# Two-layer transformer block: the first feed-forward run batch by batch, with the second attention's norm, projections and row maxima placed beside it and beside the first batch's values

## The chip, the cores and the metric

The kernel is one program on 1 core of a Trainium2 chip. The metric is the device time of one execution in microseconds, as the median of several runs. The kernel before was timed in 3 runs. A profiled execution of it gives the rows shown below.

## What is computed

Two layers work on x, 2 batches of 512 tokens by 256 features. Each layer is `x += gate * attention(norm(x))` and then `x += gate * ffn(norm(x))`, where the gates and the scale and shift of each norm come from a small vector c per batch.

```python
# layer 0 attention: 16 heads of 16, causal window of 64 tokens
scores = where(band, q @ k.T / 4, -max);  out = softmax(scores) @ v;  out @ w_out.T
# layer 0 ffn: a shared expert and 16 routed experts (4 chosen of 2 groups)
y = sum_e combine[t, e] * (silu(x @ W1[e].T) * (x @ W3[e].T)) @ W2[e].T
# layer 1 attention: 16 query heads, ONE key head and ONE value head, causal over all 512 tokens
# layer 1 ffn: a shared expert of 1024 and 8 routed experts of 128 (2 chosen)
```

All products are float32 in quality: each operand is split into a high part (rounded) and a low part (the rest), and a product is three matmuls, hi*hi, lo*hi and hi*lo.

## The kernel before

Each engine has its program written out by hand; semaphores join them. The order of the work is the order of the code, and no scheduler changes it.

**Feed-forward.** The hidden units of a layer are cut into tiles of 128: 25 tiles in layer 0, 16 in layer 1. A tile's weights are one 128x768 block. SyncE (SP) loads it into one of two raw buffers (`load_ffn`, L348), ScalarE (ACT) writes the high part (`weights_high`, L1288), GpSimd (POOL) the low part (`weights_low`, L519), and the next load into that buffer waits for the low part (`split`). A unit u is one tile for one batch. TensorE does `up(u)`, 12 matmuls of 128x512 in two halves (6 for g, 6 for u, L553), and one unit later `down(u)`, 12 matmuls of 128x256 (L994). Between them stand: ACT silu of g (L1308); VectorE (DVE) times u, which it reads from PSUM (L1783, "gu"); DVE times the combine row (L1786, "hid", both inputs in SBUF); ACT high part (L1312, "high"); DVE low part (L1790, "low"). `down(u)` waits for "low". A tile serves batch 0 and then batch 1, so the weights of a layer are loaded and split once, every second unit. The first three tiles ("early") run while the norm of batch 1 is still under way.

**After the feed-forward of layer 0.** `causal_maxima` follows: the norm of layer 1, `project1` (q, k, v), then for 32 heads (16 per batch) `scores` on TensorE (L724 and mask products L729), three row maxima on DVE (L1572) and a masked copy of q on ACT (L1160). The maxima of a batch are transposed (`max_rows`, L747), split by ACT and DVE, and stored to DRAM (L304, `store_maxima`) as two more rows of q; SP then loads q rows pair by pair of heads into four slots (L372).

**Values.** `values_pass(1)` makes, for 16 pairs of heads in three thirds each (48 steps j), `keys_major(j)` (scores with the keys on the partitions, L846, with the maximum already subtracted by those two rows), exp on ACT (L1228), and for each group of four heads four value products (L877). DVE reads a group's result, divides and transposes (L1588 to L1605), POOL makes its low part (L496), and `project_out` (L892) multiplies by the output weights. In steps of it ACT makes the high parts of the first three tiles of layer 1's feed-forward, at j = 11, 17 and 25, and SP loads the next raw tiles after the q rows of heads u = 19 and u = 23 of the list of 32 (`load_attention`).

Batch 0 and batch 1 of the maxima stand before all values, so DRAM stores and loads of batch 0 lie beside the maxima of batch 1.

## Time and profile before

| what | us |
|---|---|
| median of 3 runs | 650.18 |
| lowest and highest run | 646.22, 654.21 |
| span of the profiled execution | 648.5 |
| TensorE busy in the span | 599.5 |
| VectorE busy | 379.0 |
| ScalarE busy | 302.4 |
| GpSimd busy | 118.5 |

The profiled execution has no time of its own beside its span: 648.5 us, 1.7 under the median of the runs. Busy TensorE is not TensorE at its peak, since the ends of matmuls are modelled. PEclk is the granted clock as a share of 2.4 GHz, so 0.50 is 1.2 GHz.

### The profile page before, as it was taken

The page shows a single profiled execution, that of the slowest core. Times are in us where ns is not written, and L with a number is a line of the kernel's source. Part 1 is how long each engine was busy: PE and PEld are TensorE (multiplying, and loading weights), DVE is VectorE, ACT ScalarE, POOL GpSimd, SP SyncE. Part 2 cuts the span into 40 slices and gives each one's busy share as a digit, 9 for nine tenths or more (in the row PEclk, how much of TensorE's full clock was granted, in tenths as well). Part 3 has the DMA queues.
Part 4 walks back from the last instruction along what each step waited for, and adds up shares of the span by engine and source line. Part 5 has one row for each costly group of instructions (what it writes and reads, how often), then busy time and mean ns, then how long its engine had stood idle before and what let it go on. Part 6 is the DMA issues. An engine that isn't in the chain of part 4 may idle for free.

```text
span 648.5 us, 10714 instructions
## 1 busy us (share of the span) xinstructions
PE 599.5 (92%) x3880; PEld 470.2 (73%) x3890; DVE 379.0 (58%) x757; ACT 302.4 (47%) x466; POOL 118.5 (18%) x90
## 2 busy tenths in 40 slices
PE   3899999898999999999999797889999999999995
PEld 3778645786888888888887565544446878888885
DVE  7567757753254544454457799795376543335556
ACT  3666775463233333333342583448855643333331
POOL 4500031223022222112230000001301231222220
PEclk9998999999699999999999899899999999999999
DMA  8454674000011111111100024402310000111101
GB/s 319 123 213 135 221 215 132 1 25 24 2 36 42 45 49 49 49 49 49 49 25 1 0 71 134 127 4 77 113 40 1 25 25 25 50 49 49 48 2 65
DMA packets 22195, 44.66 MB, mean 69 GB/s; under 512 B 3632, under 2 KB 7632, under 8 KB 22160
## 3 DMA queue, kind: packets, MB, share of 16 engines
q1 hardware_dynamic: 21840, 44.05, 21.5%
q8 instruction: 23, 0.38, 0.2%
q10 hardware_dynamic: 320, 0.13, 0.1%
q14 instruction: 12, 0.10, 0.0%
HBM read 33.16 MB, written 11.01 MB: 68 GB/s over the span
## 4 chain that ended last, share of the span: by engine, by line
PE 67%; DVE 19%; ACT 6%; issue 3%; DMA 3%; POOL 1%; SPq 1%; DVEq 0%; ACTq 0%
PE PS L553 32%; PE PS L994 15%; DVE nmx L1572 5%; PE PS L877 4%; DMA qk_slot<-rows_scr 2%; PE PS L846 2%; PE PS L825 2%; PE PS L830 2%; DVE stats L1470 1%; PE PS L724 1%; DVE x L1641 1%; DVE xn L1786 1%; PE PS L892 1%; PE PS L713 1%; PE PS L561 1%
## 5 line engine op out<-in xcount | busy, mean ns | idle before, releaser
L1312 ACT ACTIVATE qk_hi<-xn 128x512 fp32r<-128x512 f32 x82 | 51.7, 631 | 170.5 <-DVE xn L1786 140.8
L553 PE MATMUL PS<-h_hi,wqkv_hi 128*128 128x512 f32 x304 | 104.4, 401 | 2.6 <-DVE h_lo L1504 1.9
L553 PE MATMUL PS<-h_hi,wqkv_lo 128*128 128x512 f32 x272 | 92.3, 395 | 1.8 <-DVE xn L1696 1.8
L1783 DVE TENSOR_TENSOR prs<-prs,PS 128x512 f32<-128x512 f32 x60 | 41.2, 687 | 88.7 <-PE PS L553 77.7
L519 POOL TENSOR_TENSOR wqkv_hi<-fw_raw,wqkv_hi 128x768 fp32r<-128x768 f32 x18 | 33.1, 1841 | 254.3 <-ACT wqkv_hi L1288 254.3
L1790 DVE TENSOR_TENSOR qk_lo<-xn,qk_hi 128x512 fp32r<-128x512 f32 x70 | 48.4, 692 | 49.1 <-ACT qk_hi L1312 49.1
L1308 ACT ACTIVATE prs<-PS 128x512 f32<-128x512 f32 x82 | 48.5, 592 | 47.3 <-PE PS L553 47.3
L553 PEld LDWEIGHTS PS<-h_hi,wqkv_hi 128*128 128x128 f32 x304 | 58.1, 191 | 15.3 <-DVE h_lo L1504 2.7
L553 PE MATMUL PS<-h_lo,wqkv_hi 128*128 128x512 f32 x160 | 63.6, 397 | 0.0
L553 PEld LDWEIGHTS PS<-h_hi,wqkv_lo 128*128 128x128 f32 x272 | 51.1, 188 | 13.3 <-DVE xn L1696 2.7
L1572 DVE TENSOR_REDUCE nmx<-PS 128x512 f32 (+4 forms) x96 | 54.2, 635 | 4.6 <-PE PS L729 4.5
L994 PE MATMUL PS<-wqkv_hi,qk_hi 128*128 128x256 f32 x280 | 52.1, 285 | 0.9 <-POOL qk_lo L525 0.7
L519 POOL TENSOR_TENSOR wqkv_lo<-fw_raw,wqkv_lo 128x768 fp32r<-128x768 f32 x16 | 29.5, 1846 | 122.4 <-ACT wqkv_lo L1288 122.4
L553 PE MATMUL PS<-h_lo,wqkv_lo 128*128 128x512 f32 x128 | 50.3, 393 | 0.0
L994 PEld LDWEIGHTS PS<-wqkv_hi,qk_hi 128*128 128x128 f32 x280 | 45.0, 188 | 5.0 <-POOL qk_lo L525 1.6
L994 PE MATMUL PS<-wqkv_lo,qk_hi 128*128 128x256 f32 x256 | 47.3, 283 | 0.7 <-DVE qk_lo L1790 0.7
L1786 DVE TENSOR_TENSOR xn<-prs,V 128x512 f32<-128x512 f32 x60 | 44.7, 745 | 2.1
L994 PEld LDWEIGHTS PS<-wqkv_lo,qk_hi 128*128 128x128 f32 x256 | 41.0, 188 | 4.0 <-DVE qk_lo L1790 1.5
L994 PE MATMUL PS<-wqkv_hi,qk_lo 128*128 128x256 f32 x140 | 39.5, 282 | 0.0
L1566 DVE TENSOR_REDUCE nmx<-PS 128x384 f32 (+1 forms) x64 | 31.1, 548 | 13.0 <-PE PS L713 12.9
L994 PE MATMUL PS<-wqkv_lo,qk_lo 128*128 128x256 f32 x128 | 36.0, 281 | 0.0
L1160 ACT ACTIVATE q_masked<-qk_hi,headmask 128x512 fp32r<-128x512 f32 (+1 forms) x48 | 32.3, 715 | 5.5 <-PE PS L729 3.5
(259 smaller groups left out, 1203.2 us busy)
## 6 DMA issues: line engine op xcount, KB each, us to landing
fw_raw<-in_ffn SPq DMA_DIRECT2D x41, 384.0 KB, 3.1
qk_slot<-rows_scr SPq DMA_DIRECT2D x32, 200.0 KB
rows_scr<-qk_hi SPq DMA_DIRECT2D x16, 256.0 KB
qk_slot<-q_scr SPq DMA_DIRECT2D x32, 100.0 KB
rows_scr<-qk_lo SPq DMA_DIRECT2D x8, 256.0 KB
wmod<-in_wmod SPq DMA_DIRECT2D x1, 1536.0 KB, 13.4
x<-in_x SPq DMA_DIRECT2D x2, 512.0 KB, 4.1
wmod<-in_wmod SPq DMA_DIRECT2D x1, 1024.0 KB, 9.6
```

The source lines that it names most:

```text
L519: nc.gpsimd.tensor_tensor(w[1], fw[s][:, :], w[0].bitcast(F32), ALU.subtract)\
L553: ins = nc.tensor.matmul(dst, left(a, c), right(b, c), start=n == 0, stop=n == total - 1)
L877: ins = nc.tensor.matmul(PS[s * VW:s * VW + rows, O_BANK[l][g % 2], kb * P:kb * P + n], v, probs[l][slot][:, col:col + n], start=kb == 0, ...
L994: ins = nc.tensor.matmul(PS[:, 2 * b + t // 2, (t % 2) * D:(t % 2 + 1) * D], hidR[u % 2 if isinstance(u, int) else b][a][:, t * P:(t + 1) ...
L1160: nc.scalar.activation(qm[s][:, :], rows[:, bass.ds(head // 2, 1), :].rearrange("p m t -> p (m t)").bitcast(F32), ACT.Copy, scale=headmask ...
L1308: nc.scalar.activation(gact[b], PS[:, 4, :], ACT.Silu).then_inc(f["silu"], 1)
L1312: nc.scalar.activation(hidR[b][0], hid[b], ACT.Copy).then_inc(f["hi"], 1)
L1566: nc.vector.tensor_reduce(nmx[:, bass.ds(NT * u + 2 * i, 2)], PS[:, 2 * h + i, 0:2 * KEYS0].rearrange("p (t k) -> p t k", k=KEYS0), X, ALU ...
L1572: nc.vector.tensor_reduce(nmx[:, bass.ds(NT * u + qt, k)], PS[:, 3 * h + bank, 0:k * w].rearrange("p (t k) -> p t k", k=w), X, ALU.max, ne ...
L1783: tt(hid[buf] if half is None else gu[buf], gact[buf], PS[:, 5, :], ALU.mult).then_inc(f["gu"], 1)
L1786: tt(hid[buf], gu[buf], cB[b][half], ALU.mult).then_inc(f["hid"], 1)
L1790: tt(hidR[buf][1], hid[buf], hidR[buf][0].bitcast(F32), ALU.subtract).then_inc(f["lo"], 1)
```

## The change

**Layer 0's feed-forward runs batch by batch.** Units 0 to 27 are the early ones and batch 0; units 28 to 49 (`TURN` = 28) are batch 1. Every unit from 6 on has another tile, so tiles 3 to 24 are loaded and split twice: 47 loads for 25. Four pairs of buffers hold split weights (`fw0R`). On ACT the high part of a tile now stands between silu and "high" of every unit.

**Batch 0 of layer 1 stands beside batch 1's units.** The gates of layer 1 come after unit 9; half outputs and the norm of batch 0 in units 28 to 33; its projections in units 33 to 35; two heads of scores and maxima in each of units 37 to 44 (`FIRST_HEADS` = 37), all in one set of three PSUM banks (0, 1, 6); `max_rows` in unit 45.

**Batch 0's values come directly after.** Beside them stand batch 1's norm transposes (j = 8), projections (j = 12, 14, 15, 16) and heads 0 to 5 of its maxima (j = 18 to 23). Heads 6 to 15 follow alone, in two sets of banks; then `max_rows`, `project_out` of batch 0, and only then batch 1's values (j = 24 to 47), which need batch 1's maxima to have gone through DRAM. `keys_major` has two pairs of PSUM banks in turn where it had three. The first three tiles of layer 1's feed-forward are now split at j = 29, 35 and 41; SP still loads raw tiles behind heads u = 19 and u = 23. All filler matmuls of this part are gone, and the loops of layer 0's feed-forward are written out.

```diff
+MAX1_BANK = [7, 5]
+SCORE1 = [[(0, 1, 6)], [(2, 3, 7), (0, 1, 4)]]
+PAIR_BANK = [0, 4]
+ALONE = 6
...
-TAIL = [3, 2]
+TAIL = 2
 EARLY = 3
 EU = 2 * EARLY
+LAST0 = 2 * TILES[0]
+TURN = EU + TILES[0] - EARLY
+FIRST_HEADS = TURN + 9
...
+        fwX = [prxR[:, a, 0:TW] for a in range(2)]
+        fw0R = [fwR[0], fwR[1], fwX, fwE[1]]
...
+        def weights(l, i):
+            if l == 0:
+                return fw0R[i % 4]
+            return fwE[i % 2] if isinstance(i, int) and (2 <= i < 4 or i > TILES[1] - TAIL) else fwR[i % 2]
...
+        def tile0(j):
+            return j if j < TILES[0] else j - TILES[0] + EARLY
+        def heads_of(u):
+            i = 2 * (u - FIRST_HEADS)
+            return (i, i + 1) if 0 <= i < H else (None, None)
+        def scored1(b, i, piece):
+            sets = SCORE1[b]
+            if b and i >= ALONE:
+                return sets[i % 2][piece]
+            return sets[0][piece]
...
+            load_attention(0, 2 * SLOTS, UNITS)
+            load_ffn_rest(0)
+            rows_at = FIRST_HEADS + 4
+            load_ffn_again(TILES[0], rows_at)
+            store_rows1(0)
+            load_ffn_again(rows_at, rows_at + 1)
+            load_keys1(0)
+            load_ffn_again(rows_at + 1, LAST0 - EARLY)
+            store_maxima(sp, 1, 0)
+            load_attention(1, 0, H)
+            store_rows1(1)
+            load_keys1(1)
+            sp.wait_ge(ff[0]["split"], LAST0 - EARLY)
             for s in range(2):
                 load_ffn(1, 0, s, s)
-            store_maxima(sp, 1, 0)
-            sp.wait_ge(at[0]["st"], UNITS)
-            load_attention(1)
...
+            def attention1():
+                for c in range(CHUNKS):
+                    if c == 2:
+                        weights_low(1, 0, 0)
+                        weights_low(1, 1, 1)
+                    elif c == 3:
+                        weights_low(1, 2, 0)
+                    out_low(1, c)
...
+            for j in range(EARLY + 1, LAST0 - EARLY):
+                weights_low(0, j, j % 2)
+            attention1()
...
-                if u >= THIRDS:
-                    pe.wait_ge(a["p"], u - THIRDS + 1)
+                if u >= 2:
+                    pe.wait_ge(a["p"], u - 1)
+                if u == 0:
+                    pe.wait_ge(k1_loaded, 16 * 4)
+                    pe.wait_ge(a["mxd"], 3 * H)
+                elif u == 1:
+                    pe.wait_ge(ff[0]["silu"], LAST0)
+                    pe.wait_ge(ff[0]["gu"], LAST0 - EU)
+                elif u == THIRDS * PAIRS // 2:
+                    pe.wait_ge(k1_loaded, 16 * 4 * B)
+                    pe.wait_ge(a["mxd"], 3 * UNITS)
...
+            def beside_first_values(j):
+                if j == 8:
+                    norm_transposes(2, (1,))
+                elif j in (12, 14, 15, 16):
+                    project1(1, {12: 2, 14: 0, 15: 1, 16: 3}[j])
+                elif j in (18, 19, 20, 21, 22, 23):
+                    if j == 18:
+                        pe.wait_ge(qhi, 4 * B + 6)
+                        pe.wait_ge(v1_taken, 2)
+                    scores1(1, j - 18)
+            def beside_last_values(j):
+                if j == 37:
+                    norm_transposes(3, (0,))
+            def values_pass1(b, beside):
+                first = b * THIRDS * PAIRS // 2
+                for j in range(first + 2 * (1 - b), first + 6):
+                    keys_major(1, j)
+                for g in range(b * BQ + 1, (b + 1) * BQ):
+                    keys_major(1, 6 * g)
+                    beside(6 * g)
+                    keys_major(1, 6 * g + 1)
+                    beside(6 * g + 1)
+                    for kb in range(NT):
+                        values(1, g - 1, (kb,))
+                        keys_major(1, 6 * g + 2 + kb)
+                        beside(6 * g + 2 + kb)
+                values(1, (b + 1) * BQ - 1, range(NT))
+            def causal_attention():
+                values_pass1(0, beside_first_values)
+                for i in range(ALONE, H):
+                    scores1(1, i)
+                max_rows(1, 1)
+                pe.wait_ge(split, 3)
+                pe.wait_ge(at[1]["ol"], OC)
+                project_out(1, 0, range(OC), True)
+                values_pass1(1, beside_last_values)
...
+            def beside_ffn0(u):
+                if u == EU + 1:
                     pe.wait_ge(cB_ready, HALVES[0] * B)
                     shifts1()
+                elif u == EU + 3:
+                    pe.wait_ge(shifts1_taken, 1)
+                    gates1(0)
+                    gates1(1)
+                elif u == TURN + 4:
+                    norm_transposes(2, (0,))
+                elif u == TURN + 5:
+                    project1(0, 2)
+                elif u == TURN + 6:
+                    project1(0, 3)
+                    project1(0, 0)
+                elif u == TURN + 7:
+                    project1(0, 1)
+                elif u == FIRST_HEADS + H // 2:
+                    max_rows(1, 0)
+            def ffn0():
+                early_ffn(0)
+                combine_table(0, 1)
+                for u in range(EU + 1, LAST0):
+                    j = u - EARLY
+                    first, second = heads_of(u)
+                    up(0, u, u // TURN, weights(0, j), j)
+                    if first is not None:
+                        if first == 0:
+                            pe.wait_ge(qhi, 4 * B + 2)
+                            pe.wait_ge(v1_taken, 1)
+                        scores1(0, first)
+                    down(0, u - 1, (u - 1) % 2, (u - 1) // TURN, weights(0, j - 1))
+                    if second is not None:
+                        scores1(0, second)
+                    beside_ffn0(u)
+                keys_major(1, 0)
+                keys_major(1, 1)
+                down_apart(0, LAST0 - 1, 1, weights(0, LAST0 - 1 - EARLY))
...
+            def beside_ffn0(u):
+                if u == EU + 1:
+                    take_shifts1()
+                elif u == EU + 4:
+                    for g in range(2):
+                        take_gate(1, g)
+                elif u == TURN + 3:
+                    normalise(2, 0)
+                elif u == TURN + 4:
+                    modulate(2, 0)
+                elif u == TURN + 5:
+                    h_high(2, 0)
+                elif u == TURN + 6:
+                    act.wait_ge(loaded["bq"], 16)
+                    act.wait_ge(loaded["bk"], 16)
+                    nc.scalar.activation(bqs[:, :], bq[:, :], ACT.Copy, scale=SCALE).then_inc(act_order, 1)
+                    act.wait_ge(act_order, 1)
+                    take_q1(0, 2)
+                elif u == TURN + 7:
+                    take_q1(0, 0)
+                elif u == FIRST_HEADS + 1:
+                    take_q1(0, 1)
+                elif u == FIRST_HEADS + H // 2 + 1:
+                    max_high(1, 0)
+                for i in heads_of(u + 1):
+                    if i is not None:
+                        if i in (0, 8):
+                            act.wait_ge(qhi, 4 * B + (2 if i == 0 else 3))
+                        mask_q(1, 0, i // SLOTS, i % SLOTS)
+            def ffn0():
+                early_ffn(0)
+                for u in range(EU, LAST0):
+                    j = u - EARLY
+                    unit_silu(0, u, u % 2)
+                    if j + 2 < LAST0 - EARLY:
+                        weights_high(0, (j + 2) // 2, j % 2)
+                    unit_high(0, u, u % 2, True)
+                    beside_ffn0(u)
+            def ffn1():
+                def unit(u, b, routed):
+                    unit_silu(1, u, b)
+                    unit_high(1, u, b, routed)
...
+            def beside_last_values(j):
+                if j in (29, 35, 41):
+                    i = (j - 29) // 6
+                    weights_high(1, i // 2, i % 2)
+                elif j == 38:
+                    modulate(3, 0)
+                elif j == 39:
+                    h_high(3, 0)
+            def attention1():
+                exp_table()
+                for j in range(THIRDS * PAIRS // 2):
+                    exponentials1(j)
+                    beside_first_values(j)
+                for i in range(8, H):
+                    mask_q(1, 1, BQ + i // SLOTS, i % SLOTS)
+                max_high(1, 1)
+                for j in range(THIRDS * PAIRS // 2, THIRDS * PAIRS):
+                    exponentials1(j)
+                    beside_last_values(j)
+                silu_table()
             act.wait_ge(loaded["headmask"], 16)
...
+            def attention_outputs1():
+                outputs(1, 0)
+                h_low(2, 1)
+                q1_low(1, 2)
+                outputs(1, 1)
+                q1_low(1, 0)
+                q1_low(1, 1)
+                take_v1(1)
+                for i in range(H):
+                    if i == 4:
+                        outputs(1, 2)
+                    elif i == ALONE:
+                        outputs(1, 3)
+                    maxima1(1, i)
+                max_low(1, 1)
+                add_output_bias()
+                for i in range(2):
+                    dve.wait_ge(y_ps, 4 + i + 1)
+                    aggregate = gate_and_add(1, 0, 0, i, Y0_BANK[1][i])
...
+            def ffn0():
+                dve.wait_ge(cB_ready, HALVES[0] * B)
+                for u in range(EU, LAST0):
+                    unit_hid(0, u, u % 2, u // TURN, u % 2)
+                    first, second = heads_of(u)
+                    if first is not None:
+                        maxima1(0, first)
+                    unit_low(0, u, u % 2)
+                    if second is not None:
+                        maxima1(0, second)
+                    if u == EU + 2:
+                        modulation1()
+                    elif EU + 5 <= u < EU + 8:
+                        gate_step(1, u - EU - 5)
+                    elif u == TURN:
```

**Where instructions stand, ScalarE in layer 0's feed-forward.** Three units each; `prs` is silu's output, `qk_hi<-xn` is "high", `<-fw_raw` is the high part of a tile. Before:

```order
L1308 ACTIVATE prs<-PS 128x512
L1312 ACTIVATE qk_hi<-xn 128x512
L1288 ACTIVATE wqkv_lo<-fw_raw 128x768
L1308 ACTIVATE prs<-PS 128x512
L1312 ACTIVATE qk_hi<-xn 128x512
L1308 ACTIVATE prs<-PS 128x512
L1312 ACTIVATE qk_hi<-xn 128x512
L1288 ACTIVATE wqkv_hi<-fw_raw 128x768
L1288 ACTIVATE qk_hi<-fw_raw 128x768
```

After, a stretch of batch 0's units:

```order
L1412 ACTIVATE prs<-PS 128x512
L1396 ACTIVATE wqkv_hi<-fw_raw 128x768
L1416 ACTIVATE qk_hi<-xn 128x512
L1412 ACTIVATE prs<-PS 128x512
L1396 ACTIVATE wqkv_lo<-fw_raw 128x768
L1416 ACTIVATE qk_hi<-xn 128x512
L1412 ACTIVATE prs<-PS 128x512
L1396 ACTIVATE prx_r<-fw_raw 128x768
L1416 ACTIVATE qk_hi<-xn 128x512
```

A tile's copy stood behind "high"; it now stands between silu and "high", and in every unit. The order of TensorE's up and down products is unchanged.

**ScalarE in layer 1's values.** `L1228` and `L1338` are exp, the copies from `fw_raw` are the first tiles of layer 1's feed-forward. Before, from the stores of batch 1's maxima on:

```order
L304 DMA q_scr<-mxT_hi 16x4x128
L304 DMA q_scr<-mxT_lo 16x4x128
L1228 ACTIVATE wmod<-PS 128x2x512 x2
L1228 ACTIVATE wmod<-PS 128x2x256
L1228 ACTIVATE wmod<-PS 128x2x512 x2
L1228 ACTIVATE wmod<-PS 128x2x256
L1288 ACTIVATE wqkv_hi<-fw_raw 128x768
L1228 ACTIVATE prs<-PS 128x2x512 x2
```

After, from batch 1's maxima on:

```order
L1289 ACTIVATE mxT_hi<-PS 64x128
L1338 ACTIVATE prs<-PS 128x2x512 x2
L1338 ACTIVATE prs<-PS 128x2x256
L1338 ACTIVATE prx<-PS 128x2x512 x2
L1338 ACTIVATE prx<-PS 128x2x256
L1396 ACTIVATE wqkv_hi<-fw_raw 128x768
L1338 ACTIVATE wmod<-PS 128x2x512 x2
```

The first tile's copy stood after 12 of 48 exps; it now stands after 30 of 48, that is after six of batch 1's.

**SyncE before the last loads of q rows.** `fw_raw` are raw tiles, `qk_slot` q rows, `q_scr<-mxT` the stores of maxima, `k` the keys. Before:

```order
L348 DMA fw_raw<-in_ffn 128x768 x2
L304 DMA q_scr<-mxT_hi 16x4x128
L304 DMA q_scr<-mxT_lo 16x4x128
L372 DMA qk_slot<-q_scr 50x512 x20
L348 DMA fw_raw<-in_ffn 128x768
L372 DMA qk_slot<-q_scr 50x512 x4
L348 DMA fw_raw<-in_ffn 128x768
L372 DMA qk_slot<-q_scr 50x512 x8
```

After:

```order
L378 DMA fw_raw<-in_ffn 128x768 x2
L334 DMA q_scr<-mxT_hi 16x4x128
L334 DMA q_scr<-mxT_lo 16x4x128
L406 DMA qk_slot<-q_scr 50x512 x4
L378 DMA fw_raw<-in_ffn 128x768
L406 DMA qk_slot<-q_scr 50x512 x4
L378 DMA fw_raw<-in_ffn 128x768
L406 DMA qk_slot<-q_scr 50x512 x8
```

The order at the end is the same: a raw tile stands ahead of the q rows of heads 20 and 24 of the list. What stands before it on ScalarE has moved.

## Rows read from the trace of the kernel before

**Rows 1.** The page: the span.
```profile
span 648.5 us, 10714 instructions
```

**Rows 2.** Windows: length, busy PE, PEld, DVE, ACT, POOL, PEclk, DMA share, GB/s.
```profile
163.43:354.34 190.91, 190.43 (x1064) 165.87 (x1066) 95.98 (x149) 65.57 (x107) 36.92 (x20) 0.97 0.12 38
354.34:376.00 21.66, 17.61 (x95) 12.09 (x95) 16.20 (x49) 13.15 (x23) 0.00 (x0) 0.92 0.00 0
376.00:434.26 58.26, 48.03 (x294) 33.76 (x294) 53.81 (x98) 26.73 (x41) 0.00 (x0) 0.97 0.31 93
434.26:498.12 63.86, 61.39 (x539) 29.21 (x540) 35.48 (x77) 46.61 (x60) 10.66 (x7) 1.00 0.20 60
```

**Rows 3.** Chain that ended last, in layer 0's feed-forward: start, us, what.
```profile
294.17 2.78 PE PS L553 x12
296.95 1.43 PE PS L994 x12
```

**Rows 4.** Timeline, causal maxima: start, us, engine, line, operation, idle before it.
```profile
384.06 0.40 PE L724 MATMUL PS<-qk_hi,q_masked 128*128 128x256 f32 x2
386.08 0.48 PE L553 MATMUL PS<-h_hi,wq_hi 128*128 128x512 f32 x1
...
400.51 6.72 DVE L1572 TENSOR_REDUCE nmx<-PS 128x2 f32<-128x512 f32 x12
...
405.14 1.95 PE L590 MATMUL PS<-wmod,o_parts 128*128 128x256 f32 x8
```

**Rows 5.** Timeline, causal maxima: key and value projection.
```profile
378.22 1.94 PE L682 MATMUL PS<-hF,wkv 128*128 128x512 f32 x4
```

**Rows 6.** Timeline, layer 0's feed-forward: a tile split every second unit.
```profile
300.03 1.85 POOL L519 TENSOR_TENSOR wqkv_lo<-fw_raw,wqkv_lo 128x768 fp32r<-128x768 f32 x1 [6.56 <-ACT wqkv_lo L1288]
...
301.99 0.69 DVE L1786 TENSOR_TENSOR xn<-prs,V 128x512 f32<-128x512 f32 x1
...
307.57 0.83 ACT L1288 ACTIVATE wqkv_hi<-fw_raw 128x768 fp32r<-128x768 f32 x1
...
308.31 0.58 ACT L1308 ACTIVATE prs<-PS 128x512 f32<-128x512 f32 x1
```

**Rows 7.** Timeline, layer 0's feed-forward: where two tiles are split in a row.
```profile
327.13 1.85 POOL L519 TENSOR_TENSOR qk_lo<-fw_raw,qk_hi 128x768 fp32r<-128x768 f32 x1
...
327.27 2.26 DVE L1786 TENSOR_TENSOR xn<-prs,V 128x512 f32<-128x512 f32 x1
...
329.57 0.63 ACT L1312 ACTIVATE qk_hi<-xn 128x512 fp32r<-128x512 f32 x1 [3.10 <-DVE xn L1786]
...
330.23 0.69 DVE L1790 TENSOR_TENSOR qk_lo<-xn,qk_hi 128x512 fp32r<-128x512 f32 x1 [0.70 <-ACT qk_hi L1312]
...
330.98 0.39 PE L994 MATMUL PS<-wqkv_lo,qk_hi 128*128 128x256 f32 x1 [0.32 <-DVE qk_lo L1790]
```

**Rows 8.** Groups of instructions, 354.34 to 498.12: the fillers (line, shapes, count, busy, mean ns, idle).
```profile
L696 PE MATMUL PS<-maskB,zeroB 128*128 128x512 bf16 x21 | 5.2, 379 | 0.3 <-issue 0.2
```

**Rows 9.** Timeline, layer 1's values: the first value product of two groups.
```profile
440.22 0.62 PE L877 MATMUL PS<-prs,V 128*32 128x512 f32 x2
...
446.80 1.07 PE L877 MATMUL PS<-wmod,V 128*32 128x512 f32 x8
```

**Rows 10.** Windows: a stretch with one group's output on VectorE.
```profile
494.00:496.75 2.75, 2.70 (x12) 2.18 (x12) 2.51 (x6) 0.60 (x1) 0.00 (x0) 1.00 0.00 0
```

**Rows 11.** Chain that ended last: maxima transposed.
```profile
412.10 0.31 PE PS L747
```

**Rows 12.** Timeline of SP: maxima stored, q rows loaded.
```profile
412.74 0.57 SPq L304 DMA_DIRECT2D q_scr<-mxT_hi  x1
...
415.25 1.06 SPq L372 DMA_DIRECT2D qk_slot<-q_scr  x3
```

**Rows 13.** DMA issues: KB each, median us to landing.
```profile
fw_raw<-in_ffn SPq DMA_DIRECT2D x41, 384.0 KB, 3.1
```

**Rows 14.** Windows: TensorE behind a wait.
```profile
415.00:417.00 2.00, 2.00 (x9) 1.43 (x9) 1.71 (x3) 1.13 (x2) 0.00 (x0) 0.50 0.22 73
```

834 lines of the change are left out of this document (391 added, 443 removed).

## The prediction

> **What bounds the kernel now.** I read the page first, then the windows by stage, then the chain that ended last, then the timelines of the places the change touches. The profiled execution spans 648.5 us [rows 1] and has no other time of its own; it lies 1.7 us (0.3%) under the median of the runs, 650.18. I make the sum against 648.5 and take the small offset as noise. About 2%, 13 us, is what a measurement of this kernel can tell from no change.
>
> The windows [rows 2] are to show one thing: who has room. In layer 0's feed-forward (first row) TensorE is busy 190.43 of 190.91 us, VectorE 95.98, half of the stretch, ScalarE 65.57, GpSimd 36.92. In the causal maxima (third row) TensorE has 48.0 of 58.26 and VectorE 53.8: VectorE is the bound there. In the values (fourth row) TensorE has 61.4 of 63.86. So the change moves work from a stage where VectorE is late into one where TensorE has not half a microsecond free. Whatever TensorE does there lengthens it one for one; only waits can be won.
>
> **Part 1: work that enters layer 0's feed-forward.** A unit is 2.78 + 1.43 = 4.21 us of TensorE [rows 3]. What is added between units, each at its duration on TensorE: 16 heads of scores, two of which take 386.08 - 384.06 = 2.02 us [rows 4], so 16 x 1.01 = 16.2; the two halves of the gates, 1.95 each [rows 4], 3.9; key and value projections, 1.94 for one of the two [rows 5] and as much taken for the other, 3.9; two q projections, each six 512-column products like half an up or a whole down in columns, 1.43, 2.9; transposes 0.9 and the row maxima's 0.3 (estimates: eight and one small products at 0.11 to 0.3). Sum 28.2. Against it stands one stall that goes: at 330.98 "down" waited 0.32 for "low" [rows 7]. I take +27.9. None of it can hide, since TensorE is full; the bounds are 26 and 30.
>
> **Part 2: the hold of "hid".** This is the least visible cost. Before, a tile's high part stood behind "high" on ScalarE and in every second unit; now it stands between silu and "high" in every unit, and GpSimd's low part of the weights follows it at once. What that does, the trace shows: with GpSimd's low part at 327.13 for 1.85 us, the product "hid" on VectorE, which reads two operands from SBUF, started at 327.27 and ended at 329.53: 2.26 us, that is until GpSimd's end plus 0.55 [rows 7]. The same product takes 0.69 when it starts at 301.99, just behind a GpSimd operation that ends at 301.88 [rows 6]. "High" followed at 329.57, "low" at 330.23, and the down product was late by 0.32. The Trainium skill (SBUF — State Buffer, "Who interferes with whom") says the same of such a product and adds that whoever issues first keeps the port for its whole instruction; by that rule it would be GpSimd that waits where "hid" begins first, and the trace of before shows no case of that, nor needs the sum one.
>
> Now the loop of a unit. Silu (0.54 to the next start), the tile's copy 0.83, a hop of 0.08, GpSimd 1.85, VectorE's 0.55 behind it, 0.04, "high" 0.58 [rows 6, 7]: 0.54 + 0.83 + 0.08 + 1.85 + 0.55 + 0.04 + 0.58 = 4.47 us, against 4.21 of TensorE. If "hid" is caught every time, each plain unit is paced by this ring: +0.26. With 28 such units that is 7 at most; I take 4, as a unit where "hid" gets in first costs nothing. A unit with two heads has 4.21 + 2.02 = 6.23 of TensorE. Its VectorE order is u's product, hid, three maxima (1.68 per head: 6.72 us for twelve [rows 4]), low, three maxima; both heads use the same three PSUM banks, so the second head's scores wait for the first's maxima, and these wait for "hid". Counted from the end of up: hid until 2.5, maxima until 4.2, low 4.9, and the second head's maxima, with its scores behind the first's end, until about 7.4. So 7.4 in place of 6.23, 8 units: +9. The norm and half outputs in units 28 to 33 are about 1 late: +1. Sum +14. Bounds: 0 (all lateness of "low" fits into the slack of one unit) and 22 (4.47 in all, 8.0 in head units, 3 for the norm).
>
> **Part 3: from the end of layer 0's feed-forward to layer 1's output projection.** Before: 498.12 - 354.34 = 143.8 us, with TensorE busy for 17.6 + 48.0 + 61.4 = 127.0 [rows 2] and waiting for 16.8. After: the 28.2 of part 1 are gone and so are the fillers, 21 instructions and 5.2 us busy [rows 8], partly in waits; that leaves 127.0 - 28.2 - 5.2 = 93.6. The rest are waits, found by laying out the new order. Batch 0's values run at 6.58 us per group of six steps (440.22 to 446.80 [rows 9]), as before, with two PSUM pairs for three; ScalarE's exp of a group takes less than that, so I cost the lost pair at 0.2 a group, 1.5. Batch 1's first scores wait until VectorE, behind a group's output of about 2.75 [rows 10] and three low parts, has taken v: 3.4. The next group's output between its heads: 2.0. Heads 6 to 15 stand alone, VectorE-bound: 10 x (1.68 - 1.01) = 6.7. Then the maxima go through DRAM: before, the transposing at 412.10 [rows 11] was followed by the stores at 412.74 and the first load of q rows at 415.25 [rows 12], 3.15 us, and with the two loads' landing, which I put at 2.5, the trip is 5.7; of it the output projection of batch 0 covers 24 products of 256 columns at 1.43 / 12, 2.9. So 2.8 stay open. Sum of waits 16.4, total 110.0: **-33.8**. What hid that trip before (batch 0's part lay beside batch 1's maxima, batch 1's beside batch 0's values) is gone for batch 1: nothing of attention 1 can run until its rows are back. Bounds: -42 (v and trip half hidden) and -24 (the two pairs cost a microsecond a group).
>
> **Part 4: SyncE's order behind ScalarE.** SyncE loads a raw tile of layer 1's feed-forward behind q rows of head 19 and then again behind 23, and this load waits for a low part on GpSimd, which waits for ScalarE's copy. Before, that copy stood after 12 of 48 exps, long before. Now it stands at j = 29, while the q rows of the pair used from j = 30 on are queued on SyncE behind the load. So when exp 29 ends: copy 0.83, 0.08, GpSimd 1.85 [rows 6, 7], the raw tile's issue, then the q rows' issue, 0.33 each (three in 1.06 [rows 12]) and landing. Landing of a raw tile is 3.1 [rows 13], but q rows need not wait for it; theirs I put at 2 to 3. Sum 0.83 + 0.08 + 1.85 + 0.4 + 0.7 + 2.5 = 6.4, less what is scored ahead (one or two steps, about nothing, because the pairs in flight are just those that ended). The same again before j = 36. Two such stalls: +13.5 with ramps. This is what is late next once TensorE has passed the round trip. Bounds: 8, if a step's work covers 2.5 each, and 16; 0 is kept as a rival.
>
> **Part 5: the clock.** Behind a wait of TensorE the granted clock reads 0.50, that is 1.2 GHz: after the wait that follows 412.10 the stretch 415 to 417 was at it [rows 14]. The fillers that stood in such waits are gone, and there are about five new waits of 2 to 6 us. A stretch of 2 us at 0.50 loses 1 us of work. New waits less old ones: +2; bounds 0 and 8.
>
> **Sum.** 27.9 + 14 - 33.8 + 13.5 + 2 = +23.6, and 648.5 + 23.6 = 672.1 us. I forecast 672.
>
> **Rivals.**
> First, SyncE's wait is hidden (ends on the other side of 2%). Place: j = 29 and 35. If q rows of the next pairs were already in their four slots when the raw load waits, part 4 costs nothing: 27.9 + 14 - 33.8 + 2 = +10.1, 658.6 us, no measurable change. It decides as soon as both stalls together are under 2.9 us. For it: four slots and 2.94 us of loads for a group. Against: the order puts the load directly ahead of the rows, and the copy behind exp 29 is fixed.
> Second, "hid" isn't held. Place: every unit of layer 0's feed-forward. If GpSimd starts after hid in each unit, part 2 costs 3 in place of 14: 661 us, within 2% or just there. For it: silu ends well before up does, so the start of GpSimd's operation falls close to the end of up and a few tenths decide. Against: rows 7, and the copy now standing before "high". The rule of exclusive ports leads to the same 661 us if VectorE is first everywhere.
> Third, both: 27.9 + 3 - 33.8 + 2 = -0.9, 647.6, no change. Only with a well hidden trip (-42) on top does it come near being faster by 2%, at 639; with the clock as before, 637.
> Fourth, the feed-forward starves. Its raw tiles now come every unit, not every second: 384 KB in 4.2 us where the stage moved 38 GB/s [rows 2]. With one load of 3.1 [rows 13], plus copy and split of 2.76, in a ring of two buffers (5.9 for two units, 8.4) there is room; but stores of q rows and keys stand in between on SyncE, and with held units TensorE stutters and its clock may sit at 1.2 GHz for units. Twenty us of half clock beside the above: +18, 690 us.
>
> **How the numbers follow.** Forecast 0.47; first rival 0.18; second 0.14; third 0.08; fourth 0.13. Faster by over 2%, with all bounds at their low end, is half of the third, 0.04. Within 2%: the rest of the third, the first, half of the second, 0.04 + 0.18 + 0.07 = 0.29. Slower: 0.67. The range takes the forecast's own spread (parts 2, 4 and 5 down by 6, 5 and 2, up by 6, 2 and 5) and reaches into the first and fourth: 653 to 690.
>
> **What would show each step.** The window from the end of the early units to the last down should be 28 + 14 = 42 us longer than before; a plain unit in it 4.3 to 4.5 and a head unit 7.4 us; "hid" rows of over 2 us in most units (part 2 wrong if they are 0.69). From there to the output projection 110 + 13.5 + 2 = 125 us (before 143.8), with an idle row before keys_major at j = 30 and at j = 36 of about 6 us, put down to the q rows' queue (part 4 wrong if absent), one of 3 us before batch 1's first scores and one before j = 24. The granted clock at 0.50 behind these. The forecast is wrong altogether if the feed-forward stretch grows by less than 32 us, or if the part behind it is shorter than 115.

## The result and the profile after

| | before | after |
|---|---|---|
| median, us | 650.6 | 692.69 |
| lowest and highest run | 646.22, 654.21 | 690.31, 699.44 |
| span of the profiled execution | 648.5 | 690.7 |
| TensorE busy | 599.5 | 613.5 |

The changed kernel is slower: ratio 1.0675, 95% interval 1.0605 to 1.0744. I had forecast 672 us with 653 to 690; the sign was right and the amount little more than half of what came, 42.1 us in the medians and 42.2 in the spans. The medians below are of all runs of a kernel, while the ratios leave out runs more than 1.5% above the fastest; for e2, where one of four lay there, the median of the other three is 675.98 us and not 677.73.

The same stages cut out of both traces. Columns as in [rows 2]. The first five stretches of after are layer 0's feed-forward from unit 7 to its last product: units 7 to 10, plain units to 29, the units with the norm and projections of batch 0 (30 to 36), the eight units with heads, the rest. The last goes on into the output projection of layer 1.

```profile
167.17:194.32 27.15, 27.15 (x145) 23.62 (x146) 13.34 (x16) 8.50 (x14) 8.47 (x5) 0.87 0.20 59
194.32:277.80 83.48, 82.78 (x459) 68.43 (x457) 65.24 (x61) 36.26 (x59) 36.55 (x20) 1.00 0.30 90
277.80:322.14 44.34, 38.46 (x211) 30.90 (x209) 30.74 (x51) 20.14 (x34) 14.01 (x8) 1.00 0.20 63
322.14:383.14 61.00, 54.49 (x322) 43.05 (x321) 50.72 (x73) 27.22 (x43) 15.89 (x9) 1.00 0.30 89
383.14:407.70 24.56, 24.52 (x146) 20.59 (x144) 15.79 (x20) 10.24 (x17) 5.53 (x3) 1.00 0.17 53
407.70:541.60 133.90, 100.93 (x706) 55.18 (x707) 69.48 (x154) 63.44 (x86) 11.68 (x7) 0.83 0.15 48
```

The feed-forward stretch is 240.5 us against 190.9 before [rows 2]: +49.6. What follows up to the output projection is 132.9 against 143.8: -10.9. (The row of before ends at the first product of the projection's second part, 498.12; after has that product at 540.58, 1.0 ahead of the end of its row.) In front of unit 7 after is 3.7 later, though the change touches nothing there; ahead of that point its trace has 10.2 us at 1.2 GHz, as e1's below has too, where before, e2, e3 and e4 have 3.4. Behind, it is 0.3 shorter. 49.6 - 10.9 + 3.7 - 0.3 = 42.1.

**Plain units.** VectorE, ScalarE and GpSimd in one, the changed kernel's timeline (answers to [rows 6, 7]):

```profile
236.18 0.58 ACT L1412 ACTIVATE prs<-PS 128x512 f32<-128x512 f32 x1
236.66 0.83 ACT L1396 ACTIVATE qk_hi<-fw_raw 128x768 fp32r<-128x768 f32 x1
237.27 0.69 DVE L1987 TENSOR_TENSOR prs<-prs,PS 128x512 f32<-128x512 f32 x1 [0.27 <-PE PS L611]
237.57 1.85 POOL L571 TENSOR_TENSOR qk_lo<-fw_raw,qk_hi 128x768 fp32r<-128x768 f32 x1 [2.51 <-ACT qk_hi L1396]
238.00 1.97 DVE L1990 TENSOR_TENSOR xn<-prs,V 128x512 f32<-128x512 f32 x1
240.00 0.63 ACT L1416 ACTIVATE qk_hi<-xn 128x512 fp32r<-128x512 f32 x1 [2.51 <-DVE xn L1990]
```

"hid" (L1990) starts 0.43 behind GpSimd and takes 1.97 instead of 0.69; it ends at 239.97, GpSimd's end plus 0.55. It takes over 1.5 us in 32 of the 44 units. The product before it (L1987), which reads one operand from PSUM, takes its 0.69 in the same shadow. TensorE's units begin at 234.23, 238.58 and 242.94 in that stretch: 4.35 each, 4.21 before [rows 3]. The rows give the ring that sets this: from silu to the start of the copy 0.48, on to GpSimd 0.91, GpSimd 1.85, 0.55 behind it, 0.03, and from "high" to the next silu (240.53) 0.53, in all 4.35.

Where "hid" gets in first, GpSimd is the longer one, and "low" runs into it (GpSimd's and VectorE's timelines):

```profile
198.50 2.37 POOL L571 TENSOR_TENSOR prx_r<-fw_raw,prx_r 128x768 fp32r<-128x768 f32 x1 [3.48 <-ACT prx_r L1396]
...
198.47 0.69 DVE L1990 TENSOR_TENSOR xn<-prs,V 128x512 f32<-128x512 f32 x1
199.86 1.56 DVE L1994 TENSOR_TENSOR qk_lo<-xn,qk_hi 128x512 fp32r<-128x512 f32 x1 [0.70 <-ACT qk_hi L1416]
```

**Units with the norm.** VectorE's long rows in the timeline:

```profile
276.85 2.33 DVE L1803 TENSOR_TENSOR x<-x,o_parts 128x512 f32<-128x512 f32 x1
...
283.44 2.19 DVE L1803 TENSOR_TENSOR x<-x,o_parts 128x512 f32<-128x512 f32 x1
...
289.72 1.84 DVE L1643 TENSOR_SCALAR rs<-rs 128x4 int32<-128x4 int32 x1
```

and all rows of GpSimd in the same stretch:

```profile
276.79 1.84 POOL L571 TENSOR_TENSOR wqkv_hi<-fw_raw,wqkv_hi 128x768 fp32r<-128x768 f32 x1 [2.51 <-ACT wqkv_hi L1396]
283.24 1.84 POOL L571 TENSOR_TENSOR wqkv_lo<-fw_raw,wqkv_lo 128x768 fp32r<-128x768 f32 x1 [4.61 <-ACT wqkv_lo L1396]
289.69 1.85 POOL L571 TENSOR_TENSOR prx_r<-fw_raw,prx_r 128x768 fp32r<-128x768 f32 x1 [4.61 <-ACT prx_r L1396]
```

Here other instructions of VectorE run into the same hold: the addition of a half output, 2.33 and 2.19, and one step of the norm on 4 numbers a row, which takes 1.84 where its like take 0.17. Each delays the product that TensorE's next half of up waits for: 1.25, 1.24 and 1.93 us.

**Units with heads**:

```profile
340.16 1.85 POOL L571 TENSOR_TENSOR prx_r<-fw_raw,prx_r 128x768 fp32r<-128x768 f32 x1 [5.84 <-ACT prx_r L1396]
...
340.88 1.67 DVE L1990 TENSOR_TENSOR xn<-prs,V 128x512 f32<-128x512 f32 x1
...
342.48 1.74 DVE L1733 TENSOR_REDUCE nmx<-PS 128x2 f32<-128x512 f32 x3
...
343.31 0.47 PE L784 MATMUL PS<-wmod_r,q_masked 128*128 128x256 f32 x2 [0.76 <-DVE nmx L1733]
```

The maxima of the first head wait for "hid", the second head's scores wait for these. Units start at 337.03 and 344.72: 7.69.

**Behind the feed-forward.** TensorE's waits from 405 to 542:

```profile
PE PS L879 <- DMA qk_slot<-q_scr: 16.2, 3, 7.6
PE PS L784 <- DVE V L1859: 4.3, 1, 4.3
PE PS L784 <- DVE nmx L1733: 3.2, 2, 1.8
PE PS L807 <- DVE nmx L1733: 2.7, 1, 2.7
PE PS L879 <- ACT prx L1338: 2.3, 4, 1.3
```

and SyncE's issues between its stores of batch 1's maxima and the loads of the rest:

```profile
493.14 0.36 SPq L378 DMA_DIRECT2D fw_raw<-in_ffn  x1
493.54 1.48 SPq L406 DMA_DIRECT2D qk_slot<-q_scr  x4
509.32 0.36 SPq L378 DMA_DIRECT2D fw_raw<-in_ffn  x1
509.72 2.99 SPq L406 DMA_DIRECT2D qk_slot<-q_scr  x8
```

SyncE sat before each raw tile until its buffer's split was done, and the q rows came behind it: TensorE waited from 489.80 to 497.37 and from 505.96 to 513.31. In and behind these waits it ran at 1.2 GHz (the figure before the last two is PEclk; answers to [rows 14]):

```profile
495.00:502.00 7.00, 4.63 (x20) 1.54 (x20) 0.00 (x0) 2.05 (x2) 0.00 (x0) 0.50 0.24 92
510.00:518.00 8.00, 4.69 (x22) 2.98 (x26) 0.00 (x0) 2.05 (x2) 0.00 (x0) 0.50 0.47 152
```

Taken microsecond by microsecond, 44 of the 134 us are at 1.2 GHz. If I count, in each, TensorE's busy time times what is missing from full clock, the work lost is 14.4 us, against 3.1 in the 143.8 us of before.

### The profile page after: what moved, and what is told of

Same layout as the page of the kernel before. It is cut to its first block, busy times and chain, and to the rows that moved or that the text cites. A ratio compares the mean times of both kernels' runs of the same rounds, so it can differ in the third digit from the quotient of the medians.

```text
span 690.7 us, 10354 instructions
## 1 busy us (share of the span) xinstructions
PE 613.5 (89%) x3859; PEld 470.6 (68%) x3866; DVE 419.4 (61%) x757; ACT 316.3 (46%) x488; POOL 162.9 (24%) x112
## 4 chain that ended last, share of the span: by engine, by line
PE 62%; DVE 22%; ACT 8%; DMA 3%; issue 2%; POOL 1%; SPq 0%; DVEq 0%; ACTq 0%; POOLq 0%
PE PS L611 28%; PE PS L1061 11%; DVE nmx L1733 5%; PE PS L910 4%; DVE xn L1990 4%; DVE prs L1987 2%; PE PS L879 2%; PE PS L847 2%; PE PS L767 2%; PE PS L852 2%; PE PS L765 2%; ACT qk_hi L1416 1%; DVE x L1803 1%; PE PS L784 1%; DMA qk_slot<-q_scr 1%
## 5 line engine op out<-in xcount | busy, mean ns | idle before, releaser
L611 PE MATMUL PS<-h_hi,wqkv_hi 128*128 128x512 f32 x232 | 80.9, 405 | 5.2 <-DVE h_lo L1660 1.7
L1990 DVE TENSOR_TENSOR xn<-prs,V 128x512 f32<-128x512 f32 x60 | 81.9, 1365 | 2.1
L1987 DVE TENSOR_TENSOR prs<-prs,PS 128x512 f32<-128x512 f32 x60 | 41.2, 687 | 65.2 <-PE PS L611 52.8
L611 PE MATMUL PS<-h_hi,wqkv_lo 128*128 128x512 f32 x216 | 75.6, 404 | 3.8 <-DVE prs L1987 1.9
L1733 DVE TENSOR_REDUCE nmx<-PS 128x2 f32<-128x512 f32 (+2 forms) x96 | 55.2, 635 | 4.1 <-PE PS L789 4.0
L611 PEld LDWEIGHTS PS<-h_hi,wqkv_hi 128*128 128x128 f32 x232 | 44.9, 194 | 15.9 <-issue 2.8
L611 PEld LDWEIGHTS PS<-h_hi,wqkv_lo 128*128 128x128 f32 x216 | 41.6, 193 | 13.8 <-DVE xn L1902 2.7
L611 PE MATMUL PS<-h_lo,wqkv_hi 128*128 128x512 f32 x124 | 49.9, 403 | 0.0
L879 PE MATMUL PS<-qk_slot,k 50*128 50x512 f32 (+3 forms) x128 | 24.5, 420 | 21.1 <-DMA qk_slot<-q_scr 16.2
L1061 PE MATMUL PS<-wqkv_hi,qk_hi 128*128 128x256 f32 x208 | 39.6, 289 | 1.2 <-POOL qk_lo L577 0.7
L879 PEld LDWEIGHTS PS<-qk_slot,k 50*128 50x128 f32 x128 | 12.1, 205 | 41.5 <-DMA qk_slot<-q_scr 16.9
L611 PE MATMUL PS<-h_hi,prx_r 128*128 128x512 f32 x104 | 34.9, 395 | 0.0
```

Source lines behind the costliest of these rows:

```text
L611: ins = nc.tensor.matmul(dst, left(a, c), right(b, c), start=n == 0, stop=n == total - 1)
L879: nc.tensor.matmul(PS[:, bank + h, col:col + n], k1[rows, b, kb * P:(kb + 1) * P], qk[s][rows, kb * P:S], start=i == 0, stop=True, skip_gr ...
L1061: ins = nc.tensor.matmul(PS[:, 2 * b + t // 2, (t % 2) * D:(t % 2 + 1) * D], hidR[buf][a][:, t * P:(t + 1) * P], w[v][:, 2 * D:], start=Fa ...
L1733: nc.vector.tensor_reduce(nmx[:, NT * u + qt:NT * u + qt + k], PS[:, scored1(b, i, piece), 0:k * w].rearrange("p (t k) -> p t k", k=w), X, ...
L1987: tt(hid[buf] if half is None else gu[buf], gact[buf], PS[:, 5, :], ALU.mult).then_inc(f["gu"], 1)
L1990: tt(hid[buf], gu[buf], cB[b][half], ALU.mult).then_inc(f["hid"], 1)
```

## The experiments

Each ratio is to the kernel before, run on the same chip; intervals are 95%. All edits but e7's start from the changed kernel; e5, e6, e8 and e9 each add to the one before. Where runs are compared by trace, "behind the feed-forward" is the stretch from the last product of layer 0's feed-forward to the first of batch 1's output projection, 128.5 us in after.

### e1: the copy of a tile behind "high"

```
                     unit_silu(0, u, u % 2)
+                    unit_high(0, u, u % 2, True)
                     if j + 2 < LAST0 - EARLY:
                         weights_high(0, (j + 2) // 2, j % 2)
-                    unit_high(0, u, u % 2, True)
```

> Edit: in layer 0's feed-forward ScalarE copies a tile's high part directly behind "high" of the unit, not ahead of it. Theory (the hold): in the changed kernel GpSimd's split starts just before "hid" and holds it to its own end; moved by 0.63 us and more it starts when "hid" is done. Then "hid" takes 0.69 instead of 1.97 in plain units, their length falls from 4.35 to 4.21 (-0.14 x 20 = -3), and the units with norm work fall by some 3. In head units "low" (two SBUF operands) stands behind three maxima, near 3.1 us after the end of up, where GpSimd would now be at work, so "low" is held in the place of "hid" and 7.68 us stay. In all -6, 687 us. Rival (the pace is the double weight stream or the order of DMAs, not the port): nothing changes, within 2 us of 692.7, even where "hid" falls to 0.69.

Measured: 683.44 us, ratio 1.0484 (1.0417 to 1.0551), 9.3 under after. Plain units fell to 4.20 to 4.21, but for those around the steps of the gates (two of 4.78 here), and the norm's seven units from 44.3 to 42.5 us. "Low" is held in head units, as expected:

```profile
329.73 1.84 POOL L571 TENSOR_TENSOR wqkv_lo<-fw_raw,wqkv_lo 128x768 fp32r<-128x768 f32 x1 [5.01 <-ACT wqkv_lo L1396]
329.83 2.29 DVE L1994 TENSOR_TENSOR qk_lo<-xn,qk_hi 128x512 fp32r<-128x512 f32 x1
```

but this hold costs less than I said: head units take 6.85, not 7.68, for the second head's scores no longer stand behind it, only its maxima do. The rival, a pace set by the doubled stream of weights, falls: the stream is unchanged. The feed-forward stretch is 10.1 shorter than in after, and the unchanged code behind it 2.9 longer (131.4), with the clock at 1.2 GHz for 54.6 us there where after has 44.4.

### e4: the copy behind all else of the unit

```
                     unit_silu(0, u, u % 2)
-                    if j + 2 < LAST0 - EARLY:
-                        weights_high(0, (j + 2) // 2, j % 2)
                     unit_high(0, u, u % 2, True)
                     beside_ffn0(u)
+                    if j + 2 < LAST0 - EARLY:
+                        weights_high(0, (j + 2) // 2, j % 2)
```

> Edit: in layer 0's feed-forward ScalarE copies a tile's high part behind "high" and behind the unit's other work, the masked copies of q for the next heads above all. Theory (the hold, with the place of every two-operand product): in head units the copy ends 4.2 us after up and GpSimd works from 4.3 to 6.2, when neither "hid" (to 1.4), "low" (3.1 to 3.8) nor the next "hid" (from 7.6) runs. Head units then fall from 7.68 to 6.9, where the single set of banks decides (8 x -0.8 = -6); plain units to 4.21 (-3); norm units by 5 together: -14 to -15, 678 us. Rival (bank set alone sets head units: the hold there is hidden): -6, 687 us, as e1.

Measured: 682.33 us, ratio 1.0457 (1.0386 to 1.0528). Head units are 6.68 (start at 342.58, next at 349.26), as the theory said for a single set of banks. The gain over e1 is not clear in the medians; one unit behind the norm became 1.0 longer (8.98 for 7.95), since the copy now stands behind 2 us of normalising on ScalarE. The total, -10.4, is some seven tenths of the -14 to -15 expected; the feed-forward stretch is 11.3 shorter, and the unchanged code behind it 4.8 longer, with 61.4 us at 1.2 GHz.

### e2: q rows ahead of raw tiles on SyncE

```
-                    if u in (H + 3, H + 7):
+                    if l == 0 and u in (H + 3, H + 7):
                         s = (u - H) // 4
                         load_ffn(l, 1, s, 2 + s)
...
             load_attention(1, H, UNITS)
+            for s in range(2):
+                load_ffn(1, 1, s, 2 + s)
```

> Edit: SyncE issues the two raw tiles of layer 1's feed-forward that stood ahead of q rows of heads 20 and 24 only behind the last q rows. Theory (SyncE's order plus clock): the waits of 7.6 and 7.4 us before steps 30 and 36 go whole (-14.9) and with them the half-clock stretches behind them, 497 to 502 and 513 to 519 in the trace, where some 5 us of work are lost: -20, 673 us. Rival A (no clock effect: the half-clock records cost nothing of their own): -15, 678 us. Rival B (q rows are late anyway, by their slots and landing): half of the waits stay, -7, 685 us.

Measured: 677.73 us, ratio 1.0383 (1.0279 to 1.0488), 15.0 under after, or 16.7 by the three runs that count. Both waits are gone. SyncE issues all sixteen loads of q rows and then the tiles (SyncE's timeline):

```profile
479.61 20.00 SPq L406 DMA_DIRECT2D qk_slot<-q_scr  x16
499.66 58.82 SPq L378 DMA_DIRECT2D fw_raw<-in_ffn  x5
```

and TensorE's waits there, 400 to 515, are led by others:

```profile
PE PS L786 <- DVE V L1861: 4.3, 1, 4.3
PE PS L786 <- DVE nmx L1735: 3.2, 2, 1.8
PE PS L809 <- DVE nmx L1735: 2.7, 1, 2.7
PE PS L881 <- ACT prx L1340: 2.5, 4, 1.3
PE PS L881 <- DMA qk_slot<-q_scr: 2.0, 1, 2.0
```

The gain is about the waits' 14.9: behind the feed-forward the trace is 13.8 shorter, and 2.8 more of its span's 16.5 lie ahead of all changed code. That is rival A's number, but not for its reason: the half-clock time did not go with the waits. The same count in this trace still gives 15.0 us of lost work, in 34 us at 1.2 GHz, half of them between 475 and 496, where TensorE's longest waits are 2.7 and 2.0.

### e3: e2 and e4 together

> Edit: e4 (copy behind everything else of the unit on ScalarE) and e2 together. Theory: both are separate stages, so the gains add: -15 and -20, 657 us, still 1% slower than the kernel before, since 28 us of work entered a full stage and the rest of attention 1 wins less than that with its new waits. Rival (a later stage takes the gain back: raw tiles of layer 1's feed-forward late, or router): 665 us or more.

Measured: 667.43 us, ratio 1.0246 (1.0183 to 1.0309). The gains of e4 (10.4) and e2 (15.0, or 16.7 by the runs that count) sum to 25.4 or 27.1, measured 25.3: separate stages, and nothing given back that the noise would let show.

### e5: v before the output

```
                 q1_low(1, 2)
-                outputs(1, 1)
                 q1_low(1, 0)
                 q1_low(1, 1)
                 take_v1(1)
+                outputs(1, 1)
```

> Edit: e3 with one change in VectorE's order: the low parts of batch 1's q and the copy of its v stand ahead of the output of the second group of values, not behind it. Theory: VectorE was idle for 8 us before that output, so the wait of 4.3 us before batch 1's first scores goes whole, and with it the half clock of 424 to 430 (3 us of work): -7, 660 us against e3's 667. Rival (the masks or the output are late instead): the wait shrinks to 2 us and moves, -2.

Measured: 661.47 us, ratio 1.0183 (1.012 to 1.0247), 6.0 under e3. The intervals overlap, but the trace agrees: behind the feed-forward 110.4 us for e3's 116.4. The wait of 4.26 is now one of 0.44, for ScalarE.

### e6: e5 with fillers

Filler products go ahead of what waits; two of the places:

```
                 for j in range(first + 2 * (1 - b), first + 6):
                     keys_major(1, j)
+                    filler(2, 6)
...
+                filler(10, 5)
                 max_rows(1, 1)
```

> Edit: e5 with filler products (some 60 of 128x512, as the kernel before had 17) in the waits of TensorE behind layer 0's feed-forward: in the two ramps of values, beside heads 3 to 5 and 6 to 15 of batch 1, before and behind its row maxima, and at steps 39 and 40. No wait is shortened by them. Theory (clock): e3's trace had 37.6 us at 1.2 GHz there, in which 16.8 us of work were lost; fillers keep the clock up, and of the 14 or so left after e5 some 8 to 10 come back, less 2 for fillers that outlast their wait: 652 us. Rival (the granted clock tells nothing of the time, or the waits are set by DVE and ACT so that a faster TensorE waits longer): fillers cost what they last beyond the waits, 0 to +4 against e5.

Measured: 658.0 us, ratio 1.0113 (1.0053 to 1.0174), single runs from 653.71 to 663.17. The median gains 3.5, less than forecast, and its interval overlaps e5's. The profiled execution is one of the long ones and still has 13.7 us at 1.2 GHz behind the feed-forward, all in one stretch, with TensorE busy for 13.5 of them.

### e7: the kernel before without its fillers

```
-                filler(6, 3)
                 norm_transposes(2, (1,))
-                filler(6, 3)
...
-                filler(4, 7)
```

> Edit: the kernel before without the 19 filler products of its second attention (two times 6, once 7 in three places), nothing else. Theory (clock): these waits are 1 to 2 us each, and their fillers keep TensorE at 2.4 GHz; without them two or three stretches of 3 us fall to 1.2 GHz: +2 to +4 us against before. Rival (before is not sensitive; only the changed kernel's longer waits lower the clock): within 1 us, or 1 us faster as the fillers' own time goes.

(The expectations of e6 and e7 miscount the fillers of before: 16 are removed here, and the eight at the end of layer 0's feed-forward stay.) Measured: 650.11 us, ratio 0.9993 (0.9959 to 1.0027). My theory was wrong here: no +2 to +4. Yet the profiled execution does show the clock down, and for longer than any wait explains, with TensorE busy (two windows in batch 0's values):

```profile
433.00:441.00 8.00, 7.87 (x42) 2.48 (x44) 4.45 (x5) 4.25 (x6) 0.00 (x0) 0.53 0.23 68
441.00:450.00 9.00, 9.00 (x52) 3.24 (x56) 1.39 (x3) 5.57 (x7) 1.82 (x1) 0.50 0.07 23
```

In that execution the part between the feed-forward and the output projection took 149.6 us for 143.8, and the parts around it were shorter, without any change in them. Single runs lie between 643.61 and 657.27. What starts and what ends such a stretch in a busy TensorE stays open.

### e8: the second head between the halves of up

```
+                        up(0, u, u // TURN, weights(0, j), j, (0,))
+                        scores1(0, last)
+                        up(0, u, u // TURN, weights(0, j), j, (1,))
...
                     down(0, u - 1, (u - 1) % 2, (u - 1) // TURN, weights(0, j - 1))
-                    if second is not None:
-                        scores1(0, second)
```

> Edit: e6, and in the head units of layer 0's feed-forward the second head's scores stand between the two halves of the next unit's up, where the first head's maxima are surely done. Theory (one set of banks sets the head units at 6.7 in place of 6.25): the wait of 0.2 to 0.7 us before the second head goes and a head unit takes 6.3 to 6.4: -2 to -3 us against e6. Rival (VectorE's two heads per unit decide, as the next first head then waits): units stay 6.7, 0.

Measured: 652.94 us, ratio 1.0067 (1.0028 to 1.0106). Head units are 6.30 (a unit's start at 331.73, the next one's at 338.03), no wait left in them. The eight head units with their scores take 50.4 us for e6's 54.4, 4.0 less; the 5.1 in the medians are not clear of noise by themselves. Behind the feed-forward e6, e8 and e9 have the same code, so their three executions show what the clock alone does there (in this order):

```profile
394.57:506.86 112.29, 104.73 (x742) 52.83 (x752) 65.22 (x147) 63.22 (x84) 10.08 (x6) 0.94 0.19 57
388.40:494.22 105.82, 98.98 (x741) 50.90 (x752) 65.23 (x147) 62.93 (x84) 10.11 (x6) 1.00 0.20 61
386.19:494.38 108.19, 102.09 (x753) 52.17 (x752) 65.40 (x147) 63.00 (x84) 10.08 (x6) 0.97 0.19 60
```

They had 13.7, 0 and 6.8 us at 1.2 GHz; lost work by the count is 6.6, 0 and 3.4, and the stretch is 6.5 and 2.4 longer than in e8. Here, with fillers in the waits, the count is nearly the time.

### e9: the norm's units

```
+                    last = heads_of(u + 1)[0] is not None
+                    if last:
+                        beside_ffn0(u)
                     if j + 2 < LAST0 - EARLY:
                         weights_high(0, (j + 2) // 2, j % 2)
...
+                    if u == TURN:
+                        aggregate = half_out(0, 0, 0, lambda: unit_low(0, u, u % 2))
```

> Edit: e8, and (a) ScalarE's copy of a tile stands behind "high" at once where no masked copies follow, so that in the unit after the norm it isn't behind 2 us of normalising; (b) VectorE takes the product of a half output with the gate from PSUM between "hid" and "low", in its 0.7 us of waiting, so that the addition behind it starts before GpSimd. Theory: e8 waits 1.30 for GpSimd at 289.4 and 0.45 + 0.3 in each of two units for VectorE; these go: -2 to -2.5 us, 650.5, level with the kernel before and no better. Rival: the addition is held all the same (1.7 us) and only (a) counts, -1.

Measured: 649.3 us, ratio 0.9978 (0.9949 to 1.0008): level with the kernel before. The norm's seven units take 39.0 us for e8's 43.5: the waits of 0.45 before the down products of the first two units and of 1.30 for GpSimd are gone. The addition isn't held (VectorE's timeline):

```profile
274.26 0.68 DVE L1831 TENSOR_TENSOR x<-x,o_parts 128x512 f32<-128x512 f32 x1
```

Here it comes first, and GpSimd is the one that takes longer (GpSimd's timeline):

```profile
274.43 2.21 POOL L573 TENSOR_TENSOR wqkv_hi<-fw_raw,wqkv_hi 128x768 fp32r<-128x768 f32 x1 [2.03 <-ACT wqkv_hi L1418]
```

2.21 in place of 1.85 from a start 0.17 behind. This is what the Trainium skill says (SBUF — State Buffer, "Who interferes with whom"): issue order, not the shape of an operation, decides who blocks. The trace of before had only one direction; after has the other in four units, as at 198.50 above.

### e10: the changed kernel with fillers alone

```
                     if j == 18:
                         pe.wait_ge(qhi, 4 * B + 6)
+                        filler(16, 2)
...
+                    if g in (BQ + 1, BQ + 2):
+                        pe.wait_ge(at[1]["p"], 6 * g - 1)
+                        filler(28, PAIR_BANK[0])
                     keys_major(1, 6 * g)
```

> Edit: the changed kernel with fillers alone in its waits behind layer 0's feed-forward (as e6, with 16 before batch 1's first scores and 28 before steps 30 and 36); all waits stay. Theory (clock): its trace had 44 us at 1.2 GHz there with 14.4 us of work lost; fillers bring back 8 to 11 of them: 683 us. Rival (a faster TensorE only waits longer, since q rows, VectorE and ScalarE set the ends): less than 4 us, 689 or more.

Measured: 685.73 us, ratio 1.0584 (1.0517 to 1.0651), 7.0 under after with nothing else changed; the intervals overlap. From the end of the feed-forward to the point that matches after's 541.60, 129.3 us at a clock of 0.99:

```profile
403.60:532.92 129.32, 121.35 (x854) 62.89 (x854) 69.45 (x154) 63.78 (x86) 11.72 (x7) 0.99 0.16 50
```

after needed 133.9 at 0.83: 4.6 less here. The other 4.1 of the 8.7 between the two spans lie ahead of this stretch, where nothing was changed. Lost work fell from 14.4 to 1.7, so 12.7 by the count came back as 4.6 in time. That is the net of what the clock gave and what fillers took where they outlast a wait; how much each was isn't shown. That a faster TensorE also only meets waits for VectorE, ScalarE and q rows sooner is likely and not shown either.

## Why the prediction fell short

**Part 1, work entering a full stage (27.9).** Right. Units 7 to 10 are 1.9 longer than the 25.3 us of before, with 3.9 of gates in them. TensorE was busy throughout in both, but its clock there was 0.80 before and 0.87 after, by the count 5.1 and 3.4 us of lost work: the gates cost nearly their length, and 1.7 of it is hidden by the clock's chance. The units with norm and projections carry 7.7 and those with heads 16.2 (e8 shows the heads bare: 6.30 - 4.21 = 2.09 for two, 2.02 said).

**Part 2, the hold (14, bounds 0 and 22).** The mechanism was right, some 1.97 us for "hid" in most units, and 4.35 a unit where I had 4.3 to 4.5. (The ring of 4.47 took 0.58 for "high" from silu's row in [rows 6]; it is 0.53 to the next silu, and silu's own piece 0.48 for 0.54. A unit where "hid" gets in first was priced at nothing; "low" is then held.) The term was mis-sized by 8. Plain units 11 to 29: 83.48 - 19 x 4.21 = 3.5 (4 said). Head units: 61.0 - 33.7 - 16.2 = 11.1 (9 said: 7.68 for 7.4). The step that failed is "the norm and half outputs in units 28 to 33 are about 1 late": 44.34 - 29.5 - 7.7 = 7.2. Together 21.8. I had looked for one instruction, "hid", and not asked which others of VectorE would meet a GpSimd that now works in every unit. The additions of the half outputs and even one tiny step of the norm were held, 1.5 to 1.7 us each, and VectorE, with 4.4 us of instructions in a unit of 4.21, had no room for it. Not all of the 21.8 is the hold. e4, which moves ScalarE's copy alone, takes about 2 from the plain units and 6.6 from the head units; e8 takes 4.0 more from the head units by giving the second head's scores another place, which is the price of the single set of banks; e9's norm units are 5.3 shorter than after's. The 3.7 that stay are mostly VectorE's steps of gates and norm.

**Part 3, from the feed-forward to the output projection (-33.8).** Right in its waits. Those of over 0.2 us, part 4's left out, sum to 17.1 where I had 16.4: v 4.3 (3.4 said), heads beside and alone 3.2 + 2.7 (8.7 said), the trip's open end 1.3 (2.8 said), and 5.6 for ScalarE's exp (1.5 said, for the lost pair of banks). So the errors of the terms cancel in part, which is luck. TensorE was busy for 99.9 us of the 132.9 where I had 93.6; these 6.3 belong to part 5.

**Part 4, SyncE behind ScalarE (13.5).** Right: waits of 7.57 and 7.35 for 6.4 each with ramps, 14.9 together, and 13.8 in e2's trace.

**Part 5, the clock (+2, bounds 0 and 8).** Mis-sized, and the second step that failed. "About five new waits of 2 to 6 us" were four of over 2, 2.7 to 7.6 long; what failed is "a stretch of 2 us at 0.50", since a stretch at 1.2 GHz lasted 3 to 14 us with its wait, 44 us in all for 7 before. TensorE's 6.3 us of extra busy time are one measure of the cost, e10's 4.6 in the trace and 7.0 in the medians two more, all over the 2 said; after's extra of 11.3 in counted work is the upper end. The removed fillers were priced at 5.2 of work saved in part 3, and named in part 5 without a price of their own. e7 shows why that was not plain: before could do without its own.

**Chance.** 3.7 us of the profiled execution's 42.2 lie ahead of all changed code.

The sum by stages, measured for said: feed-forward +49.6 (26.1 work, 21.8 of part 2, 1.7 at its end, of which 1.2 are the first two steps of scores, which now stand there) for +41.9, behind it -10.9 for -18.3, ahead +3.7 for 0, the tail -0.3 for 0. Of the rivals the first (SyncE's wait hidden), the second and the third fall with the rows above and with e2 and e1. The fourth gave nearly the right time, 690, for a wrong reason: the feed-forward did not starve, its clock was 1.00 from unit 11 on and no wait for a DMA stands in it. The range ended at 690 although parts 2 and 5 had upper bounds 14 us above what I took; both came out near these bounds at once. Nothing ties the two together in the traces, as the clock was 1.00 through the feed-forward's held units; the range took too little of either.

The idea itself comes out level. With the hold, SyncE's order, one order on VectorE, the place of a head's scores and the fillers mended, e9 stands at 0.9978 of before: the 28 us of TensorE's work put into the full feed-forward come back out of waits behind it. No version here beats the kernel before by more than its measurement is uncertain.

## What to carry to other kernels

Where a change makes GpSimd work more often, list every VectorE instruction that can meet it, not the one the last trace showed held, and place GpSimd's work by the gaps of all of them: one copy on ScalarE, put about 3 us later in its unit, was worth 9 to 10 us here. When a producer on one engine moves later, look at each in-order queue that waits for it and at what is queued behind; that cost could be worked out from durations, 13.5 us for 14.9. Work moved from a stage with waits into one without costs its full length at once and wins it back only if no new wait takes the place.
